# Second attention: the stacks of the first four head pairs straight from TensorE projections with tripled weight columns

## The reference

```
x += 0.5 * ffn0(ln(x))      dense gelu FFN + 8 experts, top 2, RMS norms
x += attn0(ln(x))           relu attention over features
x += 0.5 * ffn0(ln(x))
x += 0.5 * ffn1(ln(x))      8 relu experts, top 4
x += attn1(ln(x))           16 heads, causal, ALiBi        <- the change is here
x += 0.5 * ffn1(ln(x))
```

```
c = h @ w_dkv.T             (256 -> 128)
q = h @ w_q.T   k = c @ w_uk.T   v = c @ w_uv.T      16 heads of 16
s = (q . k) * 16**-0.5 - 0.0625 * (i - j), masked where j > i
out = softmax(s) @ v @ w_o.T
```

## Time and profile before

| | |
|---|---|
| median of 3 runs | 577.04 us (576.34 to 579.65) |
| profiled execution | 574.21 us |
| its span | 572.5 us |
| mean granted PE clock | 0.959 |
| PE busy | 510.7 us, 89% of the span |
| DVE busy | 410.7 us, 72% |
| ACT busy | 254.0 us, 44% |
| POOL busy | 126.9 us, 22% |
| DMA, mean | 43 GB/s |

### The profile page before, as it was taken

One profiled execution on the slowest core, in us unless ns is written; L12 is line 12 of the kernel. 1 busy time (PEld: TensorE's weight loads), 2 busy tenths in 40 slices (PEclk: granted clock), 3 DMA queues, 4 the chain that ended last, 5 costly groups with the idle time before them and its releaser, 6 DMA issues.

```text
span 572.5 us, 9227 instructions
## 1 busy us (share of the span) xinstructions
PE 510.7 (89%) x3106; PEld 434.5 (76%) x3106; DVE 410.7 (72%) x1215; ACT 254.0 (44%) x552; POOL 126.9 (22%) x192
## 2 busy tenths in 40 slices
PE   1999999999999999999999957985587988889995
PEld 1788888888888888888888846874466766668884
DVE  3669796754976836885886889886546877837985
ACT  3656634353225243244643622642335766444341
POOL 1001000100101100000110253480423554414351
PEclk9999999999999999999999979989569999889998
DMA  6322210000000000011000006005513530000011
GB/s 192 110 85 84 82 38 1 0 2 1 1 1 1 1 1 1 1 44 50 19 2 0 2 1 194 0 1 184 129 56 133 129 99 13 1 1 1 1 38 37
DMA packets 16718, 24.83 MB, mean 43 GB/s; under 512 B 2720, under 2 KB 11168, under 8 KB 16576
## 3 DMA queue, kind: packets, MB, share of 16 engines
q1 hardware_dynamic: 15616, 23.73, 14.0%
q10 hardware_dynamic: 1056, 0.51, 0.4%
HBM read 18.99 MB, written 5.24 MB: 42 GB/s over the span
## 4 chain that ended last, share of the span: by engine, by line
PE 73%; DVE 10%; issue 7%; ACT 4%; POOL 3%; DMA 1%; ACTq 1%; DVEq 0%; POOLq 0%
PE ps L565 21%; PE ps L567 20%; PE ps L566 20%; PE ps L888 2%; DVE gel L1379 1%; PE ps L959 1%; PE ps L848 1%; POOL al L494 1%; PE ps L575 1%; PE ps L860 1%; DVE ps L1664 1%; DMA post_b<-in_posts_dram 1%; PE ps L874 1%; DVE gel L1377 1%; DVE z L1299 1%
## 5 line engine op out<-in xcount | busy, mean ns | idle before, releaser
L565 PE MATMUL ps<-zh,w0u_h 128*128 128x512 f32 x256 | 103.3, 403 | 2.5 <-issue 2.5
L567 PE MATMUL ps<-zl,w0u_h 128*128 128x512 f32 x256 | 102.1, 399 | 0.0
L566 PE MATMUL ps<-zh,w0u_l 128*128 128x512 f32 x256 | 101.8, 398 | 0.0
L1016 ACT ACTIVATE gel<-ps 128x512 f32<-128x512 f32 x64 | 38.3, 598 | 105.3 <-PE ps L567 105.2
L1397 DVE TENSOR_TENSOR act<-gel,ps 128x512 f32<-128x512 f32 x64 | 43.8, 685 | 43.8 <-ACT gel L1016 43.6
L565 PE MATMUL ps<-w0d_h,ah 128*128 128x256 f32 x256 | 73.8, 288 | 0.4
L566 PE MATMUL ps<-w0d_h,al 128*128 128x256 f32 x256 | 72.4, 283 | 0.0
L567 PE MATMUL ps<-w0d_l,ah 128*128 128x256 f32 x256 | 72.4, 283 | 0.0
L1664 DVE CUSTOM_DVE_ANT_0 ps<-ps,bias 128x128 f32<-128x128 f32 (+1 forms) x128 | 43.1, 382 | 24.1 <-PE ps L848 23.5
L494 POOL TENSOR_TENSOR al<-act,ah 128x512 fp32r<-128x512 f32 x32 | 41.5, 1298 | 85.3 <-ACT ah L1093 84.9
L565 PEld LDWEIGHTS ps<-zh,w0u_h 128*128 128x128 f32 x256 | 48.9, 191 | 13.6 <-issue 4.4
(11 more groups left out here) (186 smaller groups left out, 1125.7 us busy)
## 6 DMA issues: line engine op xcount, KB each, us to landing
stage<-in_w_dram SPq DMA_DIRECT2D x16, 384.0 KB, 3.0
q_raw<-split_out SPq DMA_DIRECT2D x24, 128.0 KB, 2.8
k_raw<-split_out SPq DMA_DIRECT2D x48, 64.0 KB, 2.8
stage<-in_w_dram SPq DMA_DIRECT2D x8, 256.0 KB, 2.6
k_raw<-in_zeros_dram SPq DMA_DIRECT2D x1, 1536.0 KB, 11.2
x<-in_x_dram SPq DMA_DIRECT2D x2, 512.0 KB, 5.2
split_out<-qh SPq DMA_DIRECT2D x4, 256.0 KB, 2.3
split_out<-ql SPq DMA_DIRECT2D x4, 256.0 KB, 2.7
```

Of the source, the lines that this page charges most:

```text
L565: pe.matmul(o, lh, rh, start=start, stop=False, **kw)
L566: pe.matmul(o, ll, rh, start=False, stop=False, **kw)
L567: return pe.matmul(o, lh, rl, start=False, stop=stop, **kw)
L1016: nc.scalar.activation(gel[:, n % 2, :], ps[:, 2 * (n % 2), :], ACT.Gelu_apprx_tanh).then_inc(gelu_s, 1)
```

## The change

Pairs 0 to 3 (half 0 of block 0, DIRECT = 4) don't go through DRAM any more. ACT copies the columns of w_q and w_uk that belong to each of these pairs three times next to each other (hi and lo parts: `tripled(0)` in place of the second constant-rows copy in the FFN ahead, `tripled(1)` at the start of attn1). With them PE makes a projection whose 96 output rows are three copies of the pair's 32 (`direct_q`, `direct_k`, 256 columns: the first sequence). ACT writes all 96 rows of the slot rounded (`direct_hi`, for k twice with a mask of 0 and 1 as scale, one for each head), and DVE replaces the 32 rows that hold the lo part (`direct_lo`). The tripled weights lie in slots 4 to 7 until then, so the constant rows of these slots are written afterwards.

The order changes with it. Ahead of the loop stand c, direct 0 and 1 and q and k of half 1. Direct 2 and 3, q and k of half 0 and both v move into steps 0 to 5. SP writes half 1 and reads h = 1 first, then writes half 0 and reads h = 2 and 3. The last accumulation of the FFN ahead, its `finish1` and the statistics of block 1 move on DVE into steps 1 and 5, the normalisation to step 8. POOL's `ln_scale` comes first, pairs 4 to 7 at its head 2. On ACT pairs 4 to 6 are rounded after probs(1). The insertions for block 1 move by six steps: Z to 11 and 13, C to 15, Q to 17 and 21, K to 19 and 23. The pairs ahead (AHEAD), and the step in which a pair is rounded from pair 7 on, stay.

```diff
+DIRECT = 4
-Z_HALVES = (5, 7)
-C_STEP = 9
-Q_STEPS = (11, 15)
-K_STEPS = (13, 17)
+Z_HALVES = (11, 13)
+C_STEP = 15
+Q_STEPS = (17, 21)
+K_STEPS = (19, 23)
...
+        def direct_bank(a):
+            return (3, MISC_BANK, 7, 3)[a]
...
-                for m, kind in ((0, 0), (0, 1), (1, 1), (1, 0)):
-                    write(0, m, kind)
-                for h in range(4):
-                    read(h)
+                sp.dma_start(half_mask[:, :], mask_in).then_inc(mask_s, 16)
+                for m, hs in ((1, (1,)), (0, (2, 3))):
+                    write(0, m, 0)
+                    write(0, m, 1)
+                    for h in hs:
+                        read(h)
...
-                        for gp in range(HALF):
-                            round_pair(gp)
                         ln_scale(st.p + 1)
-                        for gp in range(HALF, AHEAD):
-                            round_pair(gp)
                         for hd in range(4 * HEADS):
-                            if hd % 2 == 0 and hd // 2 + AHEAD < 4 * PAIRS:
+                            if hd == 2:
+                                for gp in range(DIRECT, AHEAD + 1):
+                                    round_pair(gp)
+                            if hd and hd % 2 == 0 and hd // 2 + AHEAD < 4 * PAIRS:
                                 round_pair(hd // 2 + AHEAD)
...
-                project_q(0, 0)
-                project_k(0, 0)
-                pe.wait_ge(acc_s, E * f0 + U1 * st.d1 - 1)
+                for a in range(2):
+                    direct_q(a)
+                for a in range(2):
+                    direct_k(a)
+                project_q(0, 1)
                 project_k(0, 1)
-                project_q(0, 1)
-                project_v(0)
-                project_v(1)
                 for s in range(4 * HEADS + SUM):
                     if s < 4 * HEADS:
                         scores(s)
+                    if s < 2:
+                        direct_q(2 + s)
+                        direct_k(2 + s)
+                    if s == 2:
+                        project_q(0, 0)
+                    if s == 3:
+                        project_k(0, 0)
+                    if s in (4, 5):
+                        project_v(s - 4)
...
+            def direct_q(a):
+                if a == 0:
+                    pe.wait_ge(tri_s, 2)
+                if a == 1:
+                    pe.wait_ge(acc_s, E * f0 + U1 * blocks_before_attn1 - 1)
+                if a == 3:
+                    pe.wait_ge(d_lo, 1)
+                for kc in range(KC):
+                    split3(ps[0:K_ROWS, direct_bank(a), 0:SEQ], tri_q[0][:, kc, a, :], tri_q[1][:, kc, a, :],
+                           zh[:, kc, 0:SEQ], zl[:, kc, 0:SEQ], kc == 0, kc == KC - 1)
+
+            def direct_k(a):
+                pe.wait_ge(ch_s, 1)
+                pe.wait_ge(cl_s, 1)
+                split3(ps[0:K_ROWS, direct_bank(a), SEQ:2 * SEQ], tri_k[0][:, a, :], tri_k[1][:, a, :],
+                       ch[:, 0:SEQ], cl[:, 0:SEQ], True, True).then_inc(d_ps, 1)
...
-                if e == 0:
-                    pe.wait_ge(pair_s, hd // 2 + 1)
-                    pe.wait_ge(q_pair_s, hd // 2 + 1)
+                if e == 0 and hd // 2 < DIRECT:
+                    pe.wait_ge(d_lo, hd // 2 + 1)
+                elif e == 0:
+                    pe.wait_ge(pair_s, rounded(hd // 2))
+                    pe.wait_ge(q_pair_s, rounded(hd // 2))
...
+            def tripled(i, w):
+                for kc in range(KC):
+                    nc.scalar.activation(tri_q[i][:, kc, :, :].rearrange("p a (o r) -> p a o r", o=3), copies(w, W_Q + kc * D), ACT.Copy)
+                nc.scalar.activation(tri_k[i].rearrange("p a (o r) -> p a o r", o=3), copies(w, W_K), ACT.Copy).then_inc(tri_s, 1)
...
+                        if s == TURN + 1:
+                            for gp in range(DIRECT, AHEAD + 1):
+                                round_q(gp)
+                        if s > TURN and s % 2 == 0 and (s - TURN) // 2 + AHEAD < 4 * PAIRS:
                             round_q((s - TURN) // 2 + AHEAD)
...
+            def direct_hi(a):
+                act.wait_ge(d_ps, a + 1)
+                if a == 0:
+                    act.wait_ge(mask_s, 16)
+                nc.scalar.activation(qs[0:K_ROWS, a, :], ps[0:K_ROWS, direct_bank(a), 0:SEQ], ACT.Copy, scale=-(HD ** -0.5))
+                for e in range(2):
+                    i = nc.scalar.activation(ks[0:K_ROWS, a, e, :], ps[0:K_ROWS, direct_bank(a), SEQ:2 * SEQ], ACT.Copy,
+                                             scale=half_mask[0:K_ROWS, e:e + 1])
+                i.then_inc(d_hi, 1)
...
-                left_acc(st, 0, 2, later=True)
+                left_acc(st, 0, 2)
                 c_lo(0)
-                q_lo(0, 0)
-                k_lo(0, 0)
+                direct_lo(0)
+                q_lo(0, 1)
                 k_lo(0, 1)
-                q_lo(0, 1)
-                left_acc(st, 0, 1)
-                prepare(p + 1, 0)
+                direct_lo(1)
                 for s in range(4 * HEADS + SUM):
                     if s < 4 * HEADS:
                         bias_min(s)
+                    if s < 2:
+                        direct_lo(2 + s)
+                    if s == 1:
+                        left_acc(st, 0, 1, later=True)
+                    if s == 2:
+                        q_lo(0, 0)
...
+                    if s == 3:
+                        k_lo(0, 0)
+                    if s == 5:
+                        finish1(st.d1 - 1)
+                        prepare(p + 1, 0)
...
-                    if s == 2:
+                    if s == 8:
                         prepare(p + 1, 1)
```

More of the change, by code:

```diff
@@ L75, with program @@
 N_SETUP = 6
[L78 removed]
+def program(nc, x_in, w0, w1, wr, pre, posts, att0, r0, ident_in, cap_in, iota_in, wa, rows_in, zeros_in, mask_in, bias_in, split_out, out,
             stages=STAGES):
@@ L180, in program @@
         on = comb[:, 0:2, :]
+        ring = ks[:, DIRECT:SLOTS, :, :].rearrange("p s e q -> p (s e q)")
+        rest = qs[:, SLOTS - 2:SLOTS, :].rearrange("p s q -> p (s q)")
+        wide = DIRECT * K_ROWS
+        tri_q = [ring[:, KC * wide * i:KC * wide * (i + 1)].rearrange("p (k a m) -> p k a m", k=KC, m=K_ROWS) for i in range(2)]
+        tri_k = [v.rearrange("p (a m) -> p a m", m=K_ROWS) for v in (ring[:, 2 * KC * wide:(2 * KC + 1) * wide], rest[:, 0:wide])]
         oth, otl = [[t[:, i, :].rearrange("p (t c q) -> p t c q", t=2, c=KC) for t, i in ((a, 2), (a, 2), (a, 2), (q, 0))]
@@ L350, in q_bank @@
         def q_bank(b, m):
-            return MISC_BANK if b else 0 if m else 3
+            return MISC_BANK if b or not m else 2
         def c_bank(b):
@@ L358, in k_bank, with turn_of, stacks_of, rounded @@
         def k_bank(b, m):
-            return MISC_BANK if b or m else 1
+            return MISC_BANK if b else 1 if m else 7
         def v_bank(n):
-            return MISC_BANK if n >= 2 else 2 + n
+            return MISC_BANK if n >= 2 else 4 + n
+        def direct_bank(a):
+            return (3, MISC_BANK, 7, 3)[a]
+        def turn_of(b, m):
+            return 2 * b + (m if b else 1 - m) + 1
+        def stacks_of(h):
+            return STACKED * ((h + 1) // 2)
+        def rounded(gp):
+            return gp - DIRECT + 1
         def head(hd):
@@ L812, in project_k @@
                 pe.wait_ge(cl_s, b + 1)
+                if b == 0 and m == 0:
+                    pe.wait_ge(d_lo, 3)
                 if b:
@@ L1102, in ffn1, with constant_rows, copies @@
                             nc.scalar.activation(wa_h[:, :], wa_raw, ACT.Copy).then_inc(wah_s, 1)
-                        if fb == 1 and c in (4, 5) and "attn1" in stages:
+                        if fb == 1 and c == 4 and "attn1" in stages:
                             act.wait_ge(sel_in_s, 32)
[L1105 to L1108, removed]
+                            constant_rows(0)
+                        if fb == 1 and c == 6 and "attn1" in stages:
+                            tripled(0, wa_h)
+            def constant_rows(i):
+                slots = slice(i * SLOTS // 2, (i + 1) * SLOTS // 2)
+                nc.scalar.activation(ks[K_ROWS:P, slots, :, :].rearrange("p s e q -> p s (e q)"),
+                                     rows_raw.rearrange("p (o q) -> p o q", o=1)
+                                     .broadcast_to([P - K_ROWS, SLOTS // 2, 2 * SEQ]), ACT.Copy).then_inc(rows_s, 1)
+            def tripled(i, w):
+                for kc in range(KC):
+                    nc.scalar.activation(tri_q[i][:, kc, :, :].rearrange("p a (o r) -> p a o r", o=3), copies(w, W_Q + kc * D), ACT.Copy)
+                nc.scalar.activation(tri_k[i].rearrange("p a (o r) -> p a o r", o=3), copies(w, W_K), ACT.Copy).then_inc(tri_s, 1)
+            def copies(w, c):
+                return w[:, c:c + P].rearrange("p (a o r) -> p a o r", o=1, r=PAIR).broadcast_to([P, DIRECT, 3, PAIR])
             def half_z_hi(kc):
@@ L1140, in attn1 @@
```

(35 more changed lines are left out.)

58 lines of the change are left out of this document (37 added, 21 removed).

## The result

| | before | after |
|---|---|---|
| median, four executions each | 576.69 us | 580.59 us |
| ratio, 95% interval | | 1.0114 [1.0057, 1.0171] |
| median, second session (34 and 12 executions) | 576.99 us | 580.09 us |
| ratio of that session | | 1.0056 [1.0022, 1.0091] |
| profiled execution, its span | 574.2, 572.5 us | 576.3, 574.4 us |

The change makes the kernel slower by 3 to 4 us in the medians. The forecast was 578 us, no measurable change. With every execution counted, the means of the second session are 576.7 and 580.1 us.

A forecast was written before the change was run, and what follows sets the result against it. Bounds: PE's 9.2 us hole ahead of the second attention, the low clock after it, and a chain to pair 16 without slack. Landing +1.8, credit -2.1, clock +1.65 make +1.3 on 577.04: 578 us, range 572.5 to 582.5.

The forecast's parts named there:

- the landing: Stack for pair 16, rounded at step 26: lands at 451.6 us (450.1 to 454.1), before at 449.8; +1.8 us.
- First scores: Start of the second attention: first scores near 393.6 us, 10.6 us earlier than 404.17.
- DVE becomes the queue: Ahead of head 8: DVE's queued operations take 12.4 us, to 409.0, PE's work some 8 us, so DVE decides.
- POOL's order: Head 8's scores wait for ln_scale, two masks and the first rounded pair: 411.7 us against 416.24, 4.5 us left.
- Batch 1 chain: Block 1's projections: first half transposes at 415.7 us, 4.3 us later; 24.6 us on, last K at 440.3.
- What is given back: At head 23's transposed scores: PE works ahead while ACT waits, credit 2.1 us; PE then idle some 3 us.
- The clock behind the wait: After PE's idle stretch near 449 to 452 us: 3.3 us at half rate, 1.65 us lost.
- Sum: At head 23's transposed scores: landing +1.8, credit -2.1, clock +1.65 = +1.3 us; old and new order agree from there.
- The third rival: Pair 16 at step 26 decides fully: clock stays low, landing at 454.1 us, +4.7, total 581.7 us; chance 0.3.
- The first rival: The 4.5 us gained at head 8 stay: 572.5 us, or 569.6 with some clock loss saved; chance 0.2.

The follow-up runs named there:

- the late chain: Kernel before with only the steps of block 1's projections moved six later, as in the change, without the direct path: 581.6 us, ratio 1.0097.
- 4 ahead: Changed kernel with pairs rounded 4 instead of 6 ahead (AHEAD = 4), so pair 16 at step 30 instead of 26: 576.2 us, ratio 1.0064.
- the chain 2 earlier: Changed kernel with block 1's projections two steps earlier (Z 9 and 11, C 13, Q 15 and 19, K 17 and 21): 577.7 us, ratio 1.0046.

## Why the prediction was wrong

It had the mechanism and its place right. Of its sum the landing was too small, and one wait was left out. Everything is counted from C.

- *First scores.* Forecast 6.1 us behind C, measured 6.16. Right.
- *DVE becomes the queue*, and POOL's order makes head 8 late. Forecast 24.2, measured 24.75. Right, with half a microsecond.
- *Batch 1 chain.* This is the term that was mis-sized. I had the first half transposes at 28.2 and the last K at 52.8; they came at 29.5 and 54.5. Of the 1.6 us at the last K, 0.5 came with head 8. Another 0.7 lie between head 8 and the transposes: I had 4.0 us, set by DVE's normalisation, and it was PE that took 4.74, without a gap from 412.92 to 417.66, at half clock. The last 0.4 is the way from there to the last K (24.6 forecast, 25.0 measured). The way from the last K to the landing was right (11.3 forecast, 11.1 measured). So the stack landed 65.5 us behind C, where before had 62.4: 3.2 us later (3.16), not 1.8.
- *What is given back.* Head 23 came 1.15 us behind before, 3.16 less 2.01: up to there the credit of PE's work done ahead was right. But PE was not idle from 449 to 452, as I had it. It worked off its queue, at half clock until 451, and waited 1.28 us. And I took the order behind head 23 as the old one. It is not: ACT still had its backlog to do, and PE waited for it again ahead of head 24. This wait of 0.76 us stands in no term of the sum.
- *The clock behind the wait.* I took 1.65 us from a row of the FFN. Measured are 1.44: the part of the four steps from the product with v to head 27, 3.72 us instead of 2.28 at full clock. Right in size. It isn't a fixed price, though. Less the waits within the four steps, the clock cost some 1.4 us in after, also when run again, 2.5 with the late chain in before, 1.3 with 4 ahead, and nothing with the chain 2 earlier. In seven of the kernels the stretch was 4.86 or 4.87 us: before and six edits without the wait.
- *Sum*: 3.16 - 2.01 + 0.76 + 1.44 = 3.35 us at head 27 instead of 1.35. The medians say 3.1 and 3.9 us. The span of the profiled execution is only 1.9 us longer: C started 0.7 us later, head 63 is 2.5 us later behind C, and the part behind head 63 is 1.3 us shorter. Before has its two late stretches of half clock behind head 27, from 487.6 to 491.0 (ahead of head 63) and from 508.1 to 511.5, and after has none. One execution of each is too little to say whether this regain behind head 27 is the rule.

So the step of the prediction that failed is the landing of pair 16: +1.8 in the sum, +3.2 measured. With the second wait of PE for ACT, taken as nothing and measured at 0.8, it makes up the 2 us by which the sum of +1.3 was too small; with 1.3 the forecast stayed inside the 0.5%. The third rival (pair 16 decides fully, landing 4.3 late) names the same mechanism, and the truth lies between the two: landing 3.2 us later. I had given the landing from which it decides as 452.8; it was 453.7 (65.3 and 65.5 behind C). The first rival, that the gain of 4.5 us at head 8 stays, didn't come: the lead at head 8 was 4.0 us and was gone at pair 16. The direct path does what it was made for, first scores 6.2 us behind C instead of 16.7; that this shortens the kernel once the reads are moved is not shown.

That the late stack is the cause is shown from both sides: the late chain alone makes before slower (581.6 us against 577.0), and moving only the reads takes the wait and the time away (577.7), though the same move does nothing where the stack is on time (577.5). That the clock falls because of the wait is not shown. The two don't even always come together (the chain 2 earlier had the wait and full clock behind it), and no kernel here keeps PE busy during the wait.

## What to carry to other kernels

Ask of every step that is moved who consumes its result, and at which step: here seven insertions were moved by six steps while the consumer of the last stayed, and there was no slack between them, which showed only as one wait of 0.24 us in the profile. A gain at the head of a pipeline is worth what its next fixed meeting point lets through. And when a queue of transfers is late, look first whether each read needs all the writes ahead of it: a change in SP's order alone gave back 4.6 us in the median. Last, an engine that was held up has a backlog: ask who waits for the operations behind the late one, too.

## What the runs showed of the hardware

PE's clock fell around short waits as well as around the hole of 9.19 us. In after it was 0.50 from 403.4 to 420.4, around a wait of 2.57 us that ended at 403.92 and one of 2.00 that ended at 412.92. It fell again at 434.1 and at 444.3, in each case shortly behind a wait of 1.72 us (ended at 433.77 and 442.63). But a wait of 1.71 us that ended at 425.19 in the same trace was followed by full clock up to 434. So from the length of one wait alone a fall could not be told.

At 0.50 a matmul of the value projection (128x256) started every 0.21 us in after (450.13, 450.34, 450.55), at 1.00 every 0.12 us in before (450.15, 450.27, 450.38). From 445 to 451 PE counts as busy for 6.00 of 6.00 us: the busy column hides such a loss, and the clock column shows it.
